# Row maxima of a causal attention: two key blocks joined by a Relu on ScalarE and one sum-and-maximum on VectorE

## The reference

```
h = rmsnorm(x, ln1_w)
q = (h @ wq.T) in 4 heads of 32;  k, v = (h @ wk.T), (h @ wv.T) in 2 heads of 32
q = q * cos + rotate_half(q) * sin;  k = k * cos + rotate_half(k) * sin
k, v repeated, so that two query heads share one key head
scores = q @ k.T / sqrt(32), causal (a key behind its query counts as -1e30)
att = softmax(scores);  y = att @ v;  x = x + y @ wo.T
```

## Time and profile before

| | |
|---|---|
| median of three timed runs | 7796.72 us (7796.51 to 7797.44) |
| the profiled execution | 7795.31 us |
| its span | 7793.5 us |
| VectorE busy over the span | 5392.0 us (69%) |
| TensorE busy over the span | 4576.0 us (59%) |
| ScalarE busy over the span | 2826.5 us (36%) |
| stage of the heads | about 6308 to 6382 us from the start |
| stage of the maxima | about 6390 to 6751 us |

### The profile page before, as it was taken

One profiled execution on the slowest core, in us unless ns is written; L12 is line 12 of the kernel. 1 busy time (PEld: TensorE's weight loads), 2 busy tenths in 40 slices (PEclk: granted clock), 3 DMA queues, 4 the chain that ended last, 5 costly groups with the idle time before them and its releaser, 6 DMA issues. The chain is left out here.

```text
span 7793.5 us, 179150 instructions
## 1 busy us (share of the span) xinstructions
PE 4576.0 (59%) x57602; PEld 3112.0 (40%) x57632; DVE 5392.0 (69%) x30722; ACT 2826.5 (36%) x14714; POOL 217.1 (3%) x504
## 2 busy tenths in 40 slices
PE   4555555555555555555555555555545958899799
PEld 3444444444444444444444444444433422244344
DVE  7666666666666666666666666666646669999544
ACT  3333333333333333333333333333321000289333
POOL 0000000000000000000000000000000020000111
PEclk6555555555555555555555555555556976699899
DMA  1000000000000000000000000000001810000000
GB/s 45 14 13 14 13 14 14 12 14 13 14 14 12 14 12 14 13 13 14 13 14 13 14 14 12 14 12 14 4 2 66 280 49 0 2 1 1 24 4 5
DMA packets 93263, 164.30 MB, mean 21 GB/s; under 512 B 8711, under 2 KB 23087, under 8 KB 92337
## 3 DMA queue, kind: packets, MB, share of 16 engines
q1 hardware_dynamic: 89009, 150.47, 6.1%
q10 hardware_dynamic: 2816, 2.10, 0.1%
q0 software_dynamic: 512, 0.53, 0.0%
HBM read 146.25 MB, written 2.10 MB: 19 GB/s over the span
## 5 line engine op out<-in xcount | busy, mean ns | idle before, releaser
L431 PE MATMUL lstm_gates<-lstm_h_parts,lstm_wrec 128*128 128x1 f16 x36864 | 2075.8, 170 | 2821.3 <-DVE lstm_h_parts L576 2813.0
L431 PEld LDWEIGHTS lstm_gates<-lstm_h_parts,lstm_wrec 128*128 128x128 f16 x36864 | 1618.8, 107 | 3423.6 <-DVE lstm_h_parts L576 3412.5
L487 ACT ACTIVATE lstm_tanhs<-lstm_gates 128x3 f32<-128x3 f32 x4096 | 708.0, 173 | 2723.0 <-PE lstm_gates L431 2722.8
L431 PE MATMUL lstm_gate_o<-lstm_h_parts,lstm_wrec 128*128 128x1 f16 x12288 | 1440.7, 165 | 0.0
L576 DVE SCALAR_TENSOR_TENSOR lstm_h_parts<-lstm_tanh_o,lstm_c_pair 128x1 f16<-128x1 f32 x4096 | 646.4, 158 | 908.7 <-ACT lstm_c_pair L493 908.7
L571 DVE SCALAR_TENSOR_TENSOR lstm_terms<-lstm_tanhs 128x2 f32<-128x2 f32 x4096 | 659.3, 161 | 765.9 <-ACT lstm_tanhs L487 546.0
L595 DVE RECIPROCAL lstm_rec<-lstm_dist 128x52 f32<-128x52 f32 (+1 forms) x2560 | 1171.8, 462 | 4.2 <-issue 4.2
L493 ACT ACTIVATE lstm_c_pair<-lstm_c_pair 128x1 f32<-128x1 f32 x4096 | 639.0, 156 | 954.3 <-DVE lstm_terms L571 954.3
L431 PEld LDWEIGHTS lstm_gate_o<-lstm_h_parts,lstm_wrec 128*128 128x128 f16 x12288 | 961.1, 104 | 0.0
L454 PE MATMUL lstm_acc<-msg,lstm_wt 128*128 128x128 f32 x2048 | 780.3, 488 | 37.9 <-DVE lstm_wt L603 37.9
L582 DVE TENSOR_TENSOR lstm_h_parts<-hid_t,lstm_h_parts 128x1 f16<-128x1 f32 x4096 | 668.3, 163 | 182.1 <-DVE hid_t L578 13.0
(11 more groups left out here) (261 smaller groups left out, 4585.1 us busy)
## 6 DMA issues: line engine op xcount, KB each, us to landing
lstm_ring<-in_adj SPq DMA_DIRECT2D x256, 256.0 KB, 2.7
gnn_ring<-in_adj SPq DMA_DIRECT2D x64, 1024.0 KB, 5.3
w<-in_w SPq DMA_DIRECT2D x2, 1364.0 KB, 9.9
heads_cos<-in_cos SPq DMA_DIRECT2D x8, 256.0 KB, 3.1
heads_sin<-in_sin SPq DMA_DIRECT2D x8, 256.0 KB, 3.6
qs<-heads_q_high SPq DMA_DIRECT2D x64, 32.0 KB, 2.3
out<-x SPq DMA_DIRECT2D x8, 256.0 KB, 2.3
ks<-heads_k_high ACTq DMA_DIRECT2D x16, 64.0 KB, 2.4
```

Source lines behind the costliest of these rows:

```text
L431: return nc.tensor.matmul(o, wrec[:, w, g, :], h_parts[:, (n - 1) % NH, k:k + 1], start=False, stop=True, skip_group_check=True)
L487: nc.scalar.activation(tanhs[:, 0:3], gates[t % 2][:, i, :], ACT.Tanh, scale=unscale).then_inc(tanhs_ready, 1)
```

## The change

In a span in which both key blocks lie ahead of the group's diagonal, the two score blocks sa and sb were made in full and reduced over 1024 columns. Now TensorE makes q(ka - kb) in the first bank and sb = q kb in the second; ScalarE takes the Relu of the first bank into an SBUF buffer `more` (three of them); VectorE adds the second bank to that buffer and takes the maximum of the sums over the 512 columns in one operation with an accumulator output, since max(sa, sb) = sb + max(0, sa - sb). That covers three pairs of key blocks (NPAIR = 3). All other units stay as they were. VectorE's waits in front of such a unit are for ScalarE's part first and for TensorE's second.

The differences of keys are made in the heads. k has three buffers instead of two; after the low parts of the second group of a pair VectorE subtracts the two k, rounds the difference to fp16 and subtracts that again for the low part, and SP places the parts in a new tensor `T.kd`, with four DMAs a pair, after the placement of groups 2, 4 and 6. ScalarE's list in the maxima has the copies of line 1116 ahead of the first joined unit of the third tile of a group.

The diff, cut to its core:

```
 # split_heads
+        d = ph.sb("d", [P, G])
+        d_high, d_low = ph.sb("d_high", [P, G], F16), ph.sb("d_low", [P, G], F16)
...
+            def place_difference(p):
+                c = slice(p * G, (p + 1) * G)
+                sp.wait_ge(d_low_ready, p + 1)
+                for h in range(NKV):
+                    sp.dma_start(T.kd[h][0:2 * HD, c], d_high[2 * h * HD:2 * (h + 1) * HD, :]).then_inc(d_placed, 16)
+                    sp.dma_start(T.kd[h][rows(2), c], d_low[rows(2 * h), :]).then_inc(d_placed, 16)
...
                 place(g)
+                if g % 2 == 0 and 1 <= g // 2 <= NPAIR:
+                    place_difference(g // 2 - 1)
...
+                p = g // 2                                   # in lows(g), b = g % 2
+                if b and p < NPAIR:
+                    if p >= 1:
+                        dve.wait_ge(d_placed, 16 * 2 * NKV * p)
+                    nc.vector.tensor_tensor(d[:, :], k[(g - 1) % 3][:, :], k[g % 3][:, :], ALU.subtract).then_inc(d_ready, 1)
+                    dve.wait_ge(d_ready, p + 1)
+                    nc.vector.tensor_copy(d_high[:, :], d[:, :]).then_inc(d_high_ready, 1)
+                    dve.wait_ge(d_high_ready, p + 1)
+                    nc.vector.tensor_tensor(d_low[:, :], d[:, :], d_high[:, :], ALU.subtract).then_inc(d_low_ready, 1)
 # row_maxima
+        more = [ph.sb(f"more{i}", [P, G]) for i in range(3)]
+        doubled = [2 * c + 1 < g for g, k, h, c in units]
 # TensorE
+                if doubled[u]:
+                    nc.tensor.matmul(sc[u % 3][:, 0, :], T.qs[h][0:K, t * P:(t + 1) * P], T.kd[h // 2][0:K, c * G:(c + 1) * G],
+                                     start=True, stop=True)
+                    nc.tensor.matmul(sc[u % 3][:, 1, :], T.qs[h][0:K, t * P:(t + 1) * P],
+                                     T.ks[h // 2][0:K, (2 * c + 1) * G:(2 * c + 2) * G],
+                                     start=True, stop=True).then_inc(scored, 1)
+                    continue
 # VectorE
+                if doubled[u]:
+                    dve.wait_ge(more_ready, sum(doubled[:u + 1]))
                 dve.wait_ge(scored, u + 1)
-                nc.vector.reduce_max(part[:, k % 2, h, c:c + 1], sc[u % 3][:, 0:w, :].rearrange("p a s -> p (a s)"),
-                                     AX.X).then_inc(reduced, 1)
+                if doubled[u]:
+                    m = more[(sum(doubled[:u + 1]) - 1) % 3][:, :]
+                    nc.vector.tensor_tensor_reduce(out=m, in0=m, in1=sc[u % 3][:, 1, :], scale=1.0, scalar=LOWEST, op0=ALU.add, op1=ALU.max,
+                                                   accum_out=part[:, k % 2, h, c:c + 1]).then_inc(reduced, 1)
+                else:
+                    nc.vector.reduce_max(...)                # as before
 # ScalarE; place(g) holds the four copies of line 1116
+            pairs = [u for u in range(len(units)) if doubled[u]]
+            place(0)
+            for n, u in enumerate(pairs):
+                g, k, h, c = units[u]
+                if (k, h, c) == (2, 0, 0):
+                    place(g - 1)
+                act.wait_ge(scored, u + 1)
+                if n >= 3:
+                    act.wait_ge(reduced, pairs[n - 3] + 1)
+                nc.scalar.activation(more[n % 3][:, :], sc[u % 3][:, 0, :], ACT.Relu).then_inc(more_ready, 1)
+            place(NG - 1)
```

More of the change, by code:

```diff
@@ L827, in split_heads @@
         q, qs = ([ph.sb(f"{n}{i}", [P, G]) for i in range(2)] for n in ("q", "qs"))
-        k, ks = ([ph.sb(f"{n}{i}", [P, G]) for i in range(2)] for n in ("k", "ks"))
+        k, ks = ([ph.sb(f"{n}{i}", [P, G]) for i in range(m)] for n, m in (("k", 3), ("ks", 2)))
+        d = ph.sb("d", [P, G])
+        d_high, d_low = ph.sb("d_high", [P, G], F16), ph.sb("d_low", [P, G], F16)
+        d_ready, d_high_ready, d_low_ready, d_placed = (ph.sem(n) for n in ("d_ready", "d_high_ready", "d_low_ready", "d_placed"))
         q_high, q_low = ([ph.sb(f"{n}{i}", [P, G], F16) for i in range(2)] for n in ("q_high", "q_low"))
@@ L876, in _ @@
                 place(g)
+                if g % 2 == 0 and 1 <= g // 2 <= NPAIR:
+                    place_difference(g // 2 - 1)
+            sp.wait_ge(d_placed, 16 * 2 * NKV * NPAIR)
             for i in range(2):
@@ L944, in turn @@
                 if g >= 2:
-                    dve.wait_ge(k_low_ready, g - 1)
-                    dve.wait_ge(k_high_ready, g - 1)
                     dve.wait_ge(k_ready, g - 1)
-                nc.vector.tensor_tensor(k[b][:, :], k_plain[:, :], cos[b][:, :], ALU.mult)
+                if g >= 3:
+                    dve.wait_ge(k_low_ready, g - 2)
+                    dve.wait_ge(k_high_ready, g - 2)
+                    dve.wait_ge(d_ready, min((g - 1) // 2, NPAIR))
+                nc.vector.tensor_tensor(k[g % 3][:, :], k_plain[:, :], cos[b][:, :], ALU.mult)
                 nc.vector.tensor_tensor(ks[b][:, :], k_turned[:, :], sin[b][:, :], ALU.mult).then_inc(k_turned_by, 1)
@@ L961, in lows @@
                 dve.wait_ge(k_high_ready, g + 1)
-                nc.vector.tensor_tensor(k_low[b][:, :], k[b][:, :], k_high[b][:, :], ALU.subtract).then_inc(k_low_ready, 1)
+                nc.vector.tensor_tensor(k_low[b][:, :], k[g % 3][:, :], k_high[b][:, :], ALU.subtract).then_inc(k_low_ready, 1)
+                p = g // 2
[7 more added lines that the diff above has]
+                    nc.vector.tensor_tensor(d_low[:, :], d[:, :], d_high[:, :], ALU.subtract).then_inc(d_low_ready, 1)
             for g in range(NG):
@@ L989, in _ @@
                 pool.wait_ge(k_turned_by, g + 1)
-                nc.gpsimd.tensor_tensor(k[b][:, :], k[b][:, :], ks[b][:, :], ALU.add).then_inc(k_ready, 1)
+                nc.gpsimd.tensor_tensor(k[g % 3][:, :], k[g % 3][:, :], ks[b][:, :], ALU.add).then_inc(k_ready, 1)
                 if g >= 1:
@@ L1012, in _ @@
                 act.wait_ge(k_ready, g + 1)
-                nc.scalar.copy(k_high[b][:, :], k[b][:, :]).then_inc(k_high_ready, 1)
+                nc.scalar.copy(k_high[b][:, :], k[g % 3][:, :]).then_inc(k_high_ready, 1)
                 act.wait_ge(k_high_ready, g + 1)
@@ L1022 @@
 MAX_UNIT = 2.0 ** 15
+NPAIR = (NG - 1) // 2
+LOWEST = -3e38
 def row_maxima(nc, T):
@@ L1031, in row_maxima @@
         flat = ph.ps("flat", [2, NHEAD, G], F16)
+        more = [ph.sb(f"more{i}", [P, G]) for i in range(3)]
+        more_ready = ph.sem("more_ready")
         part = ph.sb("part", [P, 2, NHEAD, NG // 2])
@@ L1079, in _ @@
                     dve.wait_ge(neg_ready, t - 1)
+                if doubled[u]:
+                    dve.wait_ge(more_ready, sum(doubled[:u + 1]))
                 dve.wait_ge(scored, u + 1)
-                nc.vector.reduce_max(part[:, k % 2, h, c:c + 1], sc[u % 3][:, 0:w, :].rearrange("p a s -> p (a s)"),
-                                     AX.X).then_inc(reduced, 1)
+                if doubled[u]:
[3 more added lines that the diff above has]
+                else:
+                    nc.vector.reduce_max(part[:, k % 2, h, c:c + 1], sc[u % 3][:, 0:w, :].rearrange("p a s -> p (a s)"),
+                                         AX.X).then_inc(reduced, 1)
                 if h == NHEAD - 1 and c == g // 2:
@@ L1112, in _, with place @@
         def _(act):
-            for g in range(NG):
+            def place(g):
                 act.wait_ge(flat_ready, g + 1)
@@ L1738, in program @@
             T.ks = [sb3(f"ks{h}", [P, N], F16) for h in range(NKV)]
+            T.kd = [sb3(f"kd{h}", [P, NPAIR * G], F16) for h in range(NKV)]
             T.score_unit = sb3("score_unit", [P, 1])
```

## The result

The changed kernel takes 7723.89 us (median of four runs, 7722.29 to 7728.84), the kernel before 7796.72: a ratio of 0.9908, 95% interval 0.989 to 0.9925. The profiled execution took 7722.29 us, 73.0 us less than that of before.

The account below looks back on a forecast made before the run. VectorE alone was taken to bound the maxima's groups 2 to 7 (317.1 us). A gain of 76 us there and 7.8 us more in the heads took 7795.31 to 7727, plus 1.4 for the timed median: 7728 us, range 7712 to 7776.

Parts of the forecast that it names:

- The joined operation: Maxima, groups 2 to 7: each of 192 joined units costs VectorE 0.65 us, between 0.60 and 0.74.
- VectorE's own sum: Maxima, groups 2 to 7 after the change: VectorE's joined, wide and narrow units and tile ends make 220.2 us.
- Two cycles a column: Rival, maxima: joined units pass a column in two cycles, kernel slower than before, 7812 to 7832 us; chance 0.07.
- the dear operation: Rival, maxima: joined operation or the wait ahead of it makes 0.85 us a unit, 7754 us; chance 0.16.
- The ring: Maxima: VectorE waits for ScalarE's Relu through three PSUM buffers, latency 1.39 us; about 4 us lost.
- Copies and transposes: Maxima: ScalarE's copies ahead of tile 2's Relus cost 3.7 us, TensorE's transposes 3 us, over six groups.
- The tile's end: Maxima: three small VectorE operations at a tile's end move the next reduction back by 0.49 us, 24 times.
- the sum of before: Maxima, groups 2 to 7 before the change: VectorE's units and tile ends add to 312.8 us against 317.1 measured.
- The clock: Maxima: TensorE's mixed granted clock, about 0.92, lengthens the stretch from 231 to 241 us.
- The heads: Stage of the heads: SP issues 12 more DMAs, 0.648 us each, 7.8 us, all on the path.
- the high clock: Rival, maxima: TensorE stays at 2.4 GHz throughout, stretch 231 us, kernel 7718 us; chance 0.18.
- The low clock: Rival, maxima: TensorE stays at 1.2 GHz, stretch 280 us, kernel 7768 us; chance 0.12.

Follow-up runs that it names:

- the earlier wait: Changed kernel with ScalarE waiting for the matmul of the difference alone, by its own semaphore, not for both matmuls of the unit: 7716.78 us.
- the other order: Changed kernel with VectorE's two waits swapped, TensorE's part named first and ScalarE's second: 7726.56 us.
- the run with all three edits: Changed kernel: ScalarE waits for the difference matmul alone, GpSimd issues the differences' placements, copies follow each head's last Relu in the third tile: 7700.48 us.
- the kernel with the heads alone: Changed kernel with the differences of keys made and placed but no unit joined, maxima as before: 7805.29 us beside 7796.70 for the kernel before.
- the run with GpSimd: Changed kernel with GpSimd instead of SP issuing the twelve DMAs of the differences: 7718.09 us.

## Why the prediction was right, step by step

The forecast was 7728 us, 4.1 above the median. Its mechanism held: the maxima are VectorE's, a joined unit costs it about half a wide one, ScalarE's Relus run beside it, SP's issues come on top. Its terms:

1. *The joined operation.* I took 0.65 us, between 0.60 and 0.74. It is 0.605 (0.60 to 0.61), the lower end: the accumulator read hides whole. 192 x 0.045 = 8.6 us; VectorE's own sum is 211.6 us, not 220.2. This is the largest error of the sum. "Two cycles a column" is out with 684 ns, and so is the dear operation: neither the second operand nor the accumulator costs anything beside the product of the earlier trace rows.

The other terms of the stretch can be read from the same profile: each start of VectorE is set against the one before it and its pace (0.605 us for a joined or a narrow unit, 1.132 for a wide one, 0.49 more at a tile's end), and what comes later than that is put down to its place.

2. *The ring.* Its latency was right: in group 6 VectorE frees a buffer at 6589.71 + 0.68 = 6590.39 and starts the unit three on at 6591.73, 1.34 us against my 1.39. Its loss was not: 4 us said, 8.5 won back with the earlier wait. I had set the ring against the sum of three units of VectorE, and so left out the heads in which one of the three is wide, and group 2 altogether. But a wide unit frees its buffer late as well. What VectorE has to cover the latency with is the two units behind the release, and two short ones cover 2 x 0.605 - 0.08 = 1.13 us. The turn of group 7 shows it: the wide reduction frees its buffer at 6664.54 + 1.22 = 6665.76, and the third joined operation starts 1.33 us later. So 3 operations of group 2, 10 of group 4, 10 of group 6 and 12 of group 7 come 0.20 us late, 7.0 us in all. Groups 3 and 5, where a wide unit always stands among the two, lose nothing so. What else the earlier wait won lies where the matmuls run at 1.2 GHz and the ring is longer. That VectorE stands at ScalarE's wait, named first, is no loss: the other order is the dearer one.

3. *Copies and transposes.* 3.7 us said for the copies, 2.9 measured: 0.85 where I had 0.88, in the even groups, and next to nothing in two of the odd ones. For the transposes I allowed 3 us; the first operation of a second tile comes 2.2 us later over the six groups than that of a fourth, 1.3 of them in group 2, where the kernel before lost 1.1 in the same place, and 0.9 in the run with all three edits.

4. *The tile's end.* It was misread. In the earlier trace rows the sixteen reductions end at 6690.40 + 18.19 = 6708.59, so the next would have started at 6708.51 without the three small operations. They move it back by 0.60 us, not 0.49, and that is 2.6 of the 4.3 us by which the sum of before fell short of 317.1. After the change it is 1.28 - 0.61 = 0.67 us, and 24 x 0.18 = 4.3 us more than the sum has.

5. *The clock.* I allowed 10 us for a clock of about 0.92; it came to 0.94. Inside the tiles fourteen operations come later than by the ring's 0.20 us, all of them behind matmuls that last 0.6 us, at 1.2 GHz: 5.9 us.

So the stretch: 211.6 + 7.0 + 2.9 + 2.2 + 4.3 + 5.9 = 233.9, against 234.9 measured and 241 said; most of the rest is the rounding of the paces. That the forecast came so near is in part luck, since errors of both signs stand in the sum: the cheaper operation (-8.6), the clock (-4.1), copies and transposes (-1.6) stand against the ring (+3.0) and the tile's end (+4.3).

6. *The heads.* 7.8 us said; 8.6 in the medians of the kernel with the heads alone, 6.6 in the profile after. The term was right for SP's run of issues, which is 57.1 - 49.0 = 8.1 us longer. That it had no lower end was not: the run begins 1.5 us earlier. That VectorE's nine new operations don't hold SP up shows in the run with GpSimd: they are still there, and SP ends where it did before.

Of the rivals the high clock (7718) came nearest; the measured clock lies between it and the forecast, and the time too. The low clock was far off. The Trainium skill's rule that puts relu on VectorE (ScalarE: Activation LUTs, Rules for kernel authors), for a lead that it gives for bf16, would have been the wrong guide in this place: a Relu of 597 ns on an engine with nothing to do made room for a second operation that VectorE starts every 0.605 us, and VectorE's busy time fell by 94 us in the stretch.

## What to carry to other kernels

Where one engine fills a stage and another is idle, half of its work can move, even at the same price per element. But the path through both engines is then a ring over the PSUM buffers. With three buffers its latency, from a buffer's release to its next use, must be set against the two units that VectorE still has to do behind that release, group by group, and with nothing else queued in front of it: waiting for the one matmul that the Relu reads, and moving the copies out of its way, were worth 14 us more. An edit that needs more DMAs should be issued from a queue that doesn't end its stage.

## What was not expected of the hardware

- The accumulator read behind the joined operation (83 ns) starts with the next operation and takes no time from VectorE; the 0.605 us between starts is that of a plain product of the same size (0.60 in the earlier trace rows).
- Of two waits in front of an operation, the order counts where the engine stands at one of them: 0.03 us from the Relu's end to VectorE's start with that wait named first, 0.14 with it named second.
- A granted clock of 0.97 instead of 0.60 left a stage that VectorE bounds unchanged, 317.0 us to 317.1; a clock of 0.75 in a stage bounded by the ring lengthened each turn by 2.19 - 1.76 = 0.43 us where it stood at 1.2 GHz.
- Executions of the changed kernel differ by 3.3 us in this stretch (234.9 and 238.2), with a clock of 0.94 and 0.91. The longer one has 27 operations that come late behind matmuls at 1.2 GHz, 10.0 us in all, the shorter one 14, 5.9 us; what lowers the clock there no run tells.
